# Fusion attention rewritten as a longer, unrolled pipeline, with products of ones on TensorE around the stages

## What is computed

```python
h = image_branch(x)                                   # (64, 128, 64): three convolutions, norms, projection
h = concatenate([h, text_branch(x_txt)], axis=1)      # (64, 77, 64): 4 transformer layers -> h is (64, 205, 64)
z = layernorm(h)
q, k, v = heads(z @ Wq.T + bq), heads(z @ Wk.T + bk), heads(z @ Wv.T + bv)   # 4 heads of 16
attn = softmax(einsum('bhnd,bhmd->bhnm', q, k) * 0.25)
out = einsum('bhnm,bhmd->bhnd', attn, v).reshape(64, 205, 64).astype(bfloat16).astype(float32)
h = h + out @ Wo.T + bo                               # the fusion attention
h = h + experts(layernorm(h))                         # 8 experts, the one with the highest gate counts
```

## Time and profile before

| | us |
|---|---|
| median of 3 runs | 2439.25 (2419.43 to 2443.64) |
| the profiled execution, time | 2400.28 |
| its span (first to last instruction) | 2398.5 |
| PE busy | 2091.4 (87%) |
| DVE busy | 1799.1 (75%) |
| ACT busy | 1472.5 (61%) |
| POOL busy | 1198.4 (50%) |
| mean granted clock of TensorE | 0.944 of full |

### The profile page before, as it was taken

One profiled execution on the slowest core, in us unless ns is written; L12 is line 12 of the kernel. 1 busy time (PEld: TensorE's weight loads), 2 busy tenths in 40 slices (PEclk: granted clock), 3 DMA queues, 4 the chain that ended last, 5 costly groups with the idle time before them and its releaser, 6 DMA issues. The chain is left out here.

```text
span 2398.5 us, 61351 instructions
## 1 busy us (share of the span) xinstructions
PE 2091.4 (87%) x19889; PEld 1736.8 (72%) x19889; DVE 1799.1 (75%) x5716; ACT 1472.5 (61%) x3226; POOL 1198.4 (50%) x1518
## 2 busy tenths in 40 slices
PE   6999999947999999999999981688888885999998
PEld 6999999846888888888888871566666664666665
DVE  4655555345888888888888875688888883888888
ACT  2222222102888888888888874567666665666663
POOL 3433333213777777777777755344444433433441
PEclk8999999975999999999999995699999996999999
DMA  2000003000000000000000000000000000000000
GB/s 89 14 14 14 19 25 68 5 1 1 2 3 2 3 2 3 2 2 2 2 2 2 2 2 0 1 0 0 0 0 0 0 0 1 10 9 11 9 9 11
DMA packets 39663, 20.58 MB, mean 9 GB/s; under 512 B 29508, under 2 KB 38852, under 8 KB 39366
## 3 DMA queue, kind: packets, MB, share of 16 engines
q1 hardware_dynamic: 39466, 18.00, 3.1%
HBM read 14.63 MB, written 3.36 MB: 8 GB/s over the span
## 5 line engine op out<-in xcount | busy, mean ns | idle before, releaser
L439 PE MATMUL im_c<-im_a_hi,im_w 128*128 128x256 f32 (+2 forms) x1920 | 427.9, 317 | 14.5 <-POOL im_a_lo L349 14.5
L439 PEld LDWEIGHTS im_c<-im_a_hi,im_w 128*128 128x128 f32 x1920 | 321.0, 190 | 31.5 <-POOL im_a_lo L349 14.7
L439 PE MATMUL im_c<-im_a_lo,im_w 128*128 128x256 f32 (+2 forms) x960 | 303.0, 316 | 0.0
L1041 POOL TENSOR_TENSOR tx_KB<-tx_KF,tx_head_rows 128x1248 fp32r<-128x1248 f32 x128 | 290.4, 2268 | 23.3 <-PE tx_scores_t L1326 15.2
L343 POOL TENSOR_TENSOR im_rstd<-im_var_eps,im_power 128x4 f32<-128x4 f32 x64 | 68.7, 1073 | 286.7 <-DVE im_var_eps L278 286.7
L902 DVE TENSOR_REDUCE tx_mpad<-tx_scores 77x8 fp32r<-77x616 f32 x256 | 202.1, 790 | 2.6 <-PE tx_maxT L1314 1.9
L272 DVE BATCH_NORM_STATS2 im_stats<-im_h 128x6 f32<-128x128 f32 (+1 forms) x192 | 47.6, 303 | 190.7 <-ACT im_h L384 111.1
L439 PEld LDWEIGHTS im_c<-im_a_lo,im_w 128*128 128x128 f32 x960 | 182.7, 190 | 8.4
L1172 ACT ACTIVATE tx_PT<-tx_scores_t 77x624 f32<-77x624 f32 x256 | 176.2, 688 | 16.8 <-PE tx_scores_t L1326 4.6
L1326 PE MATMUL tx_scores_t<-tx_QP,tx_KB 128*77 128x78 f32 x2048 | 184.0, 240 | 0.0
L1326 PEld LDWEIGHTS tx_scores_t<-tx_QP,tx_KB 128*77 128x77 f32 x2048 | 172.3, 150 | 9.1 <-issue 0.3
(11 more groups left out here) (308 smaller groups left out, 6096.9 us busy)
## 6 DMA issues: line engine op xcount, KB each, us to landing
im_x<-x SPq DMA_DIRECT2D x16, 384.0 KB, 3.4
out<-h_img SPq DMA_DIRECT2D x32, 64.0 KB
tx_toks<-x_txt SPq DMA_DIRECT2D x1, 1925.0 KB
im_raw<-L_tok_conv_w SPq DMA_DIRECT2D x1, 1280.0 KB, 8.7
out<-h_txt SPq DMA_DIRECT2D x32, 38.5 KB
im_raw<-L_tok_conv_w SPq DMA_DIRECT2D x1, 960.0 KB, 4.8
im_raw<-L_tok_conv_w SPq DMA_DIRECT2D x1, 640.0 KB, 5.9
tx_raw_W<-L_txt_W SPq DMA_DIRECT2D x2, 256.0 KB, 6.5
```

The source lines that it names most:

```text
L439: last = pe.matmul(acc[:, :, d0:d1], w[c][:, slot, part], img[:, b0_:b1_, d0 + shift:d1 + shift, kj:kj + J], start=opens, stop=closes)
L1041: pool.tensor_tensor(KB[:, q % 2, t], KF[:, t].bitcast(F32).unsqueeze(1).broadcast_to([P, HPT, QW]), head_rows[:].unsqueeze(2).broadcast_t ...
```

## The change

1. `Warm`: a tile `warm_rows` (128 x 512, bfloat16, ones; set by POOL in `constants`) and `run(pe, bank, times)`, which multiplies it `times` times into a PSUM bank that nothing reads before it is written again. It is called:
   - text setup: 40 before the first embedding, 3 after each of the 16 quads, into a bank `tx_spare`;
   - text loop: 24 before each of the steps 0 and 1, 4 before each `score` of the first two quads (8 times), 20 after each of the last three steps;
   - the block of the final norm: 10 x 14 in a hardware loop;
   - attention: 60 after the weights are turned in the setup block, 12 before each of the steps -4, -3, -2;
   - experts: 36 in the setup block, 10 before each of the steps -7 to -1.
2. `h_img` and `h_txt` become two views of one tile `h` (128 x 64 samples x 2 x 64); rows 64 to 127 of the second half are cleared by POOL in the image stage's setup block (`below_text`), so that both tiles of a sample can be handled by one instruction.
3. `fusion_attention` is rewritten: biases come in through two more rows of x and of the low weights (`xT1`, `A_BIAS`); k and q are made whole, one ACT and one DVE instruction each; `KB` is gone, since scores are now products over the 64 rows of one head, with head j of a tensor in bank j; `maxT` lies in a bank of `scores`; normalising moves from ACT to POOL; `set_v` and `add_y` are one instruction each; samples are in flight over one more step, every engine's order is new, and the loop of 70 steps is unrolled.

```diff
+    def run(self, pe, bank, times):
+        for _ in range(times):
+            pe.matmul(bank, self.rows[:, 0:P], self.rows[:], start=True, stop=True)
...
-        KB = sb("KB", [P, 2, A_TENSORS, A_HPT, SEQP], F32R)
+        k_low, q_low = sb("k_low", [P, A_TENSORS, SEQP], F32R), sb("q_low", [P, A_TENSORS, SEQP], F32R)
+        maxT = scores[:, 0, 0:WIDE].rearrange("p (t s) -> p t s", t=A_TENSORS)
...
             @block.vector
+                def cut_k(m):
+                        dve.wait_ge(k_low_set, m + 1)
+                        if m >= 2:
+                            dve.wait_ge(scored_t, (m - 1) * 2)
+                        dve.tensor_tensor(KF[:, m % 2], k_rows, k_low[:].bitcast(F32), ALU.subtract).then_inc(k_cut, 1)
...
+                def add_y(m):
+                        dve.tensor_tensor(both_tiles(m), both_tiles(m), v_and_y[:], ALU.add).then_inc(y_added, 1)
...
+                def step(n):
+                    find_max(n + 1, 0)
+                    add_y(n - 2)
+                    row_stats(n + 4)
+                    find_max(n + 1, 1)
+                    cut_k(n + 2)
+                    join_max(n + 1)
+                    mean_and_var(n + 4)
+                    cut_q(n + 2)
+                    normalise_o(n)
+                    set_v(n + 1)
...
             @block.gpsimd
-                            pool.tensor_tensor(KB[:, par, t],
+                def step(n):
+                    cut_x(n + 3)
+                    deviation(n + 4)
+                    norm_rows_of(n + 4)
...
             @block.scalar
+                def step(n):
+                    exp(n, 1)
+                    low_k(n + 2)
+                    copy_out(n)
+                    low_q(n + 2)
+                    hi_x(n + 3)
+                    set_oT(n - 1)
+                    exp(n + 1, 0)
+                    set_xT(n + 3)
...
             @block.tensor
+                def take(bank, read, count):
+                    if bank in held:
+                        pe.wait_ge(*held[bank])
+                    held[bank] = (read, count)
...
+                def project(m, rows, wgt, made):
                     for t in range(A_TENSORS):
+                        pe.matmul(rows[:, t], wgt[:, 0, cols], xT[:, m % 2], start=True, stop=False)
+                        last = pe.matmul(rows[:, t], wgt[0:BIAS_ROWS, 1, cols], xT1[:, m % 2], start=False, stop=True)
...
+                def score(m, tile):
+                        for t in range(A_TENSORS):
+                            for j in range(A_HPT):
+                                head = slice(j * A_GROUP, (j + 1) * A_GROUP)
+                                last = pe.matmul(scores[0:n, j, t * SEQP:(t + 1) * SEQP], QF[head, m % 2, t, at:at + n],
+                                                 KF[head, m % 2, t], start=True, stop=True)
...
+                def score_t(m, tile):
+                                last = pe.matmul(scores_t[0:n, j, t * SEQP:(t + 1) * SEQP], KF[head, m % 2, t, at:at + n],
+                                                 QP[head, m % 2, t], start=True, stop=True)
...
+                def step(n):
+                    if n < -1:
+                        warm.run(pe, scores_t[:, 0], 12)
+                    project_k(n + 2)
+                    project_o(n - 2)
+                    score(n + 1, 1)
+                    weigh(n)
+                    project_q(n + 2)
+                    turn_max(n + 1)
+                    turn_outs(n)
+                    turn_o(n - 1)
+                    score_t(n + 1, 0)
+                    project_v(n + 1)
+                    turn_x(n + 3)
+                    score(n + 2, 0)
+                    score_t(n + 1, 1)
+
+                for n in range(-4, B + 2):
+                    step(n)
```

More of the change, by code:

```diff
@@ L1437, in text_branch, with _ @@
         with nc.Block() as block:
+            @block.tensor
+            def _(pe):
+                with pe.Fori(0, 10):
+                    warm.run(pe, scores_t[:, 0], 14)
             @block.vector
@@ L1549, in load @@
                 q.dma_start(self.raw[:, k, half * D:(half + 1) * D], wts[m]).then_inc(self.loaded, 16)
-        q.dma_start(self.bv[:], on_all_rows(wts["bv"])).then_inc(self.loaded, 16)
         q.dma_start(self.bo[D:D + 1], row(wts["bo"])).then_inc(self.loaded, 16)
[L1552 to L1559, removed]
+        for r in A_BIAS:
+            for k, m in enumerate(("bq", "bk")):
+                heads = self.b_raw[r:r + 1, k * A_HALF:(k + 1) * A_HALF].rearrange("a (h g) -> a h g", g=A_GROUP)
+                src = wts[m].rearrange("(a h c) -> a h c", a=1, c=A_DH)
+                for copy in range(3):
+                    q.dma_start(heads[:, :, copy * A_DH:(copy + 1) * A_DH], src).then_inc(self.loaded, 16)
+            q.dma_start(self.b_raw[r:r + 1, 2 * A_HALF:], row(wts["bv"])).then_inc(self.loaded, 16)
 def set_scale(pool, neg_mean, var_eps, power, rstd, neg_mean_rstd, var_ready, rstd_ready, scale_ready, m):
@@ L1671, in _ @@
                     last.then_inc(turned, 1)
+                    warm.run(pe, scores_t[:, 0], 60)
                 @block.vector
@@ L2039, in _, with turn_x @@
-                each_step(pe, step)
+                held = {}
+                def take(bank, read, count):
+                    if bank in held:
+                        pe.wait_ge(*held[bank])
+                    held[bank] = (read, count)
+                def turn_x(m):
+                    if live(m):
+                        pe.wait_ge(x_cut, m + 1)
+                        take("x_and_k", xT1_set, m + 1)
+                        for tile, (at, n) in enumerate(TILES):
+                            last = pe.transpose(x_and_k[:, at:at + n], xs[0:n, tile].bitcast(F32), ident[0:n, 0:n])
+                        last.then_inc(x_turned, 1)
@@ new lines, in project_o @@
+                def project_o(m):
+                    if live(m):
+                        pe.wait_ge(oT_set, m + 1)
+                        take("v_and_y", y_added, m + 1)
+                        for tile, (at, n) in enumerate(TILES):
+                            for part in range(2):
+                                last = pe.matmul(v_and_y[0:n, tile], oT[:, at:at + n], wo[:, part],
+                                                 start=part == 0, stop=part == 1)
+                        last.then_inc(y_made, 1)
```

615 lines of the change are left out of this document (284 added, 331 removed).

## The result

The changed kernel takes 2554.28 us (median of four runs, 2531.66 to 2560.06) beside 2429.34 for the kernel before: a ratio of 1.058, 95% interval 1.045 to 1.071. It is slower by 5.8%, where I had forecast 2387. A ratio compares the runs of each kernel that lie near its fastest, while a median is over all of its runs. e1 to e4 ran on one chip, e5 to e8 on a second, e9 to e11 on a third and e12 on a fourth, so differences across these groups are a little less sure.

A forecast was written before the change was run, and what follows sets the result against it. Attention was taken as bound by short waits between PE and its helpers, not an engine's limit. Profiled 2400.3 - 85 (loop) + 33.5 (products of ones) = 2348.8; with 39 carried over, 2387 us, held for 2355 to 2415, all cases 2335 to 2425.

The forecast's parts named there:

- Clock at full from the attention's first sample: Attention loop: the profile would show TensorE at full clock from its first sample on.
- The waits: PE's waits for DVE and ACT in an attention step: 1.96 us before, 0.25 us left after the reordering.
- Half rows side by side, 0.30 us a block: Attention scores: four products over half the rows overlap, 0.30 us a block, 1.2 for four; bounds 0.27 and 0.53.
- the prediction's own sign: Profile, block of four score products: under 0.5 us from first start to last end; 0.7 refutes the halves.
- Rival 2: Attention scores: row halves do not run side by side; four blocks cost 1.95, step 6.65, total 2431 us; chance 0.12.
- Six borders, 0.9 us a step: Attention step on PE: six new changes of the array's division at 0.15 us each; bounds 0 to 2.0 us.
- Rival 3: Attention step: borders cost more than halves save, 0.34 us each, step 7.75, total about 2500 us; chance 0.06.
- Step 5.95, bounds 5.5 to 7.3: One attention loop step, from PE's 5.7 us of work plus 0.25 of waits, against 7.25 before.
- The products of ones, +33.5 us: Cost of all products of ones over constants, embeddings, text, attention setup and experts, summed to +33.5 us.
- Hidden ones: Text setup's 40 products and the final norm's 140 lie beside other engines' work and cost 0.
- Rival 1: Products of ones cost nothing, lying in waits; costs fall to about 5, total 2359 us; chance 0.22.
- 39 us carried over unexplained: The old runs' median lies 39 us above the profiled execution; added to 2348.8 to give 2387.

The follow-up runs named there:

- e1: The changed kernel with every product of ones taken out, memsets kept: 2499.21 us, 1.035 of the kernel before.
- e4: The changed kernel with all score and score_t products over 128 rows, both heads of a pair summed (other numbers computed): 2363.76 us, 0.977 of the kernel before.
- e5: The changed kernel, products of ones kept, scores over 128 rows against k masked with zeros, result right: 2362.52 us, 0.975 of the kernel before.
- e8: The changed kernel with three products of ones ahead of each score_t block, six a step: 2442.31 us, 1.010 of the kernel before.
- e9: The changed kernel without products of ones, scores over half rows, bias products and output projection zero-filled to 128 rows: 2304.14 us, 0.940 of the kernel before.
- e11: e6 with only the text setup's 40 products of ones and the final norm's 140 put back: 2322.15 us.
- e12: The changed kernel, products of ones kept, with bias products and output projection zero-filled to 128 rows: 2354.48 us, 0.974 of the kernel before.
- e6: The changed kernel with scores over 128 rows against zero-masked k and no products of ones: 2322.21 us, 0.959 of the kernel before.
- e2: All products of ones, but with the attention of the kernel before: 2461.48 us over twelve runs, 1.009 of the kernel before.
- e10: e6 with masked keys in the score products alone, score_t back on half rows: 2328.86 us, 0.949 of the kernel before.

## Why the prediction was wrong

**The step that failed** is none of the sum's terms but what stood under all of them: "Clock at full from the attention's first sample". I took every duration of the loop from the old loop at full clock and never asked whether the new one would be granted it. The clock's fall stood in the sum at nothing, and it measured 191 us. The page's clock line said where the clock was low, and I read it as a matter of seams. The rewrite replaces products over 128 rows (with masked keys) by products over 64, and gives the low parts of k, q and v products over 97. With those, clock 0.50 and 9.24 us a step; with full rows in the scores 6.00; with the rows filled up elsewhere 5.70. That rows decide is shown, by e4, e5 and e12 against the changed kernel and by e9 against e1. How many are enough is not, nor why the clock changes in the middle of a loop.

The Trainium skill (TensorE: Matmul & The Clock Gate, "Part 1: The HAM clock gate") ties TensorE's clock to how busy it has been, and names idle time as what lowers it. The traces here don't bear this out alone: busy 329.19 of 332.00 us at 0.50, busy 316.58 of 340.00 at 0.99 in e9. Nor do stretches at the same level of the clock differ in PE's busy share: at 1.00 the changed kernel was busy 15.93 of 17.10 us (93%) and then lost it, e9 was as busy and kept it (93%, the line below), and the old loop kept it with 84%.

```profile
1602.60:1859.00 256.40, 238.55 (x2612) 182.37 (x2610) 218.34 (x585) 188.88 (x405) 95.66 (x226) 1.00 0.01 2
```

Point by point:

- *The waits* of 1.96 us fell to 0.75, read as in the earlier trace rows (two rows of e9: 23.4 us for DVE's q and 10.6 for ACT's x in 45 steps). The forecast had 0.25.
- *Half rows side by side, 0.30 us a block* held: 0.31 to 0.32 where no border follows, against 0.62 over full rows. By the prediction's own sign, first start to last end of a block, it is 0.47 at full clock ("under 0.5"), and 0.68 in e5 ("0.7 refutes"). Rival 2, no overlap, is refuted; four full-row blocks cost 2.12, where it had put 1.95.
- *Six borders, 0.9 us a step* was too high: blocks and borders come to 1.52 + 0.31 = 1.83 together, 2.12 forecast. Rival 3 is refuted at full clock. The Trainium skill (TensorEngine Tiling (Array Packing), "Key Properties") has the array drained at a change of mode; a border shows here as about 0.1 us. In e8 the block of score tile 0 takes 0.41 us up to a product of ones, and 0.32 up to the half-row block in the changed kernel.
- *Step 5.95, bounds 5.5 to 7.3*: 5.70 where the clock is full. The error is -0.25 x 63 = -16 us, to the good. That it is so small is partly luck: the waits are 0.5 us longer and PE's own work, 5.70 - 0.75 = 4.95 us against 5.7, is 0.75 shorter. Blocks and borders account for 0.3 of this.
- *The products of ones, +33.5 us*: 40.3. Text setup and filling 13.5 forecast, 14.2 measured; text to attention 9.5 and 13.9; experts 10.5 and 12 to 13. Hidden ones: 0 and 0. Rival 1, that they cost nothing, is refuted. A product lasts 30.38/140 = 0.217 us at full clock (0.24 forecast) and 4.02/9 = 0.447 at half (0.45):

```profile
1473.31 30.38 PE L72 MATMUL tx_scores_t<-warm_rows 128*128 128x512 bf16 x140 [0.42 <-PEq L881]
1515.62 0.66 PE L1707 MATMUL at_x_and_k<-ident,at_raw 64*128 64x64 f32 x4 [11.94 <-PEq L60]
1516.21 4.02 PE L72 MATMUL at_scores_t<-warm_rows 128*128 128x512 bf16 x9
```

- *39 us carried over unexplained* from the profiled execution to the median. This does not come with every kernel: e6's four runs lie within 2 us. By the inference above it belonged to the old loop, which loses its clock in some samples (shown in e2). It should have been a question: runs of one kernel that differ by 40 us already hinted that something in it had two speeds.
- The sum for a profiled execution: 2348.8 + 191 for the loop + 7 for the products = 2547, against 2548.89.

What would have been needed is a fourth rival, "the loop loses its clock", priced from the trace: the old loop's own first samples at low clock took 10.1 and 8.6 us (the lines below, of the kernel before), and PE's 5.3 us of work a step, doubled, give 10.6 us at most. From 6.8 us a step on the change loses.

```profile
1524.33 1.01 DVE L1739 TENSOR_REDUCE at_mpad<-at_scores 128x4 fp32r<-128x820 f32 x1 [1.09 <-PE at_scores L1908]
...
1534.40 1.01 DVE L1739 TENSOR_REDUCE at_mpad<-at_scores 128x4 fp32r<-128x820 f32 x1 [1.09 <-PE at_scores L1908]
...
1542.97 1.01 DVE L1739 TENSOR_REDUCE at_mpad<-at_scores 128x4 fp32r<-128x820 f32 x1 [0.16 <-PE at_scores L1908]
```

## What to carry to other kernels

When a rewrite makes matrix products span fewer rows to save time, check the granted clock of that stretch before trusting any duration: a loop can be 99% busy and run at 1.2 GHz. Filling such products up to 128 rows with zeros cost no time here and was worth 195 us (e9 against e1); full-height products of ones inside the loop also brought the clock back when there were six a step, but cost their own time, and outside it they only cost. A change's expected durations hold at the clock at which they were read, so state the clock as a term of the forecast, with its own chance and price.

## What the runs showed of the hardware that was not expected

- TensorE at a busy share of 0.99 was granted half clock for hundreds of microseconds (329.19 of 332.00 us at 0.50), where its score products spanned 64 rows and others 97 and 65. The number of rows decided, with the same instructions and columns; rows that were zero in one operand did as well as filled ones. Rows are not the whole of it: the old loop, with its scores over 128, lost the clock in e2 as well.
- The same loop can be at either level: in the changed kernel three of 63 steps took 5.7 us and nearly all others 9.2; in e10 and e12 the first samples were slow and all later ones fast. What lifts the clock in the middle of an unchanged loop stays open.
- Two 64-row products in the two halves of the array did give a factor of two (0.31 to 0.32 us for a block of four, 0.62 over full rows), but a step won only 0.3 us by it: a border to full-row products cost about 0.1, and the step has six.
- A product over 128 rows took as long as one over 97 or 65: e9's step of 5.70 us is the changed kernel's at full clock.
